# Scattering weighted expert results into one running sum instead of gathering them back by slot

## The reference

```python
xn = _layernorm(x, axis=-1)
x = x + attention(xn) + ffn(xn)
# ffn:
scores = einsum('btd,ed->bte', x, gate_w)
topk_scores, topk_idx = top_k(scores, 2)
topk_probs = softmax(topk_scores)
total_probs = sum(one_hot(topk_idx, E) * topk_probs[..., None], axis=-2)
h12 = einsum('btd,ehd->bteh', x, w12); h1, h2 = halves of h12
expert_out = einsum('bteh,edh->bted', silu(h1) * h2, w3)
y = sum(total_probs[..., None] * expert_out, axis=-2)
```

## Time and profile before

| | |
|---|---|
| median of 3 runs | 712.34 us (712.1 to 715.86) |
| the profiled execution | 713.24 us |
| its span, first to last instruction | 711.5 us |
| mean granted TensorE clock | 0.978 of full speed |
| batches 0 and 1, routing: until | 157.4 us |
| expert stage: until | about 514 us |
| attention of batches 2 to 7: until | 711.5 us |

### The profile page before, as it was taken

One profiled execution on the slowest core, in us unless ns is written; L12 is line 12 of the kernel. 1 busy time (PEld: TensorE's weight loads), 2 busy tenths in 40 slices (PEclk: granted clock), 3 DMA queues, 4 the chain that ended last, 5 costly groups with the idle time before them and its releaser, 6 DMA issues.

```text
span 711.5 us, 17988 instructions
## 1 busy us (share of the span) xinstructions
PE 633.2 (89%) x5916; PEld 512.0 (72%) x5917; DVE 571.6 (80%) x906; ACT 513.7 (72%) x883; POOL 280.4 (39%) x330
## 2 busy tenths in 40 slices
PE   0786776978999999999999999999889899999995
PEld 0564554754888888888888888888767676666673
DVE  4958899975688888888888888888687979788884
ACT  4554477474687787787777777777667788888885
POOL 3000273031344444444444444444300336666654
PEclk9998788998999999999999999999999999999999
DMA  9895477581111111111111111112168687885840
GB/s 300 268 257 174 128 262 273 146 284 31 49 53 52 59 52 52 59 53 50 59 55 50 57 56 51 56 54 56 45 161 258 174 259 180 271 227 161 215 138 30
DMA packets 66384, 92.74 MB, mean 130 GB/s; under 512 B 6448, under 2 KB 53424, under 8 KB 66320
## 3 DMA queue, kind: packets, MB, share of 16 engines
q1 hardware_dynamic: 57904, 70.56, 33.3%
q0 software_dynamic: 6864, 18.75, 7.9%
q10 hardware_dynamic: 1568, 2.76, 1.2%
HBM read 59.06 MB, written 32.83 MB: 129 GB/s over the span
## 4 chain that ended last, share of the span: by engine, by line
PE 63%; DVE 14%; ACT 10%; issue 8%; DMA 2%; POOL 2%; ACTq 0%; SPq 0%; DVEq 0%; POOLq 0%
PE PS L1300 55%; PE PS L1549 4%; DVE SMALL L964 4%; ACT WORK L781 3%; DVE XN L1122 2%; PE PS L1527 2%; DVE WALL L958 2%; ACT QS L776 1%; DMA XN<-in_x 1%; DVE WORK L1033 1%; DVE WORK L1026 1%; POOL OTS L595 1%; ACT WORK L719 1%; DVE WALL L982 1%; DMA KS<-parts_scratch 1%
## 5 line engine op out<-in xcount | busy, mean ns | idle before, releaser
L367 DVE TENSOR_TENSOR WS<-WALL,WS 128x1024 fp32r<-128x1024 f32 x136 | 166.9, 1227 | 56.0 <-ACT WS L862 41.5
L1300 PE MATMUL PS<-WS,XTS 128*128 128x512 f32 x804 | 203.9, 402 | 0.0
L1300 PEld LDWEIGHTS PS<-WS,XTS 128*128 128x128 f32 x804 | 146.2, 189 | 30.5
L862 ACT ACTIVATE WS<-WALL 128x1024 fp32r x136 | 143.7, 1056 | 9.1 <-issue 0.3
L1300 PE MATMUL PS<-DOWN_HIGH,HTS 128*128 x568 | 108.3, 290 | 5.0 <-DVE DOWN_LOW L958 3.5
L595 POOL TENSOR_TENSOR OTS<-SIDE,XN 128x256 f32<-128x256 f32 x31 | 23.8, 768 | 209.2 <-DVE XN L1122 142.2
L1300 PEld LDWEIGHTS PS<-DOWN_HIGH,HTS 128*128 128x128 f32 x568 | 86.4, 190 | 5.5 <-issue 5.5
L964 DVE TENSOR_REDUCE SMALL<-PS 128x8 f32<-128x1024 f32 x64 | 77.5, 1211 | 12.6 <-PE PS L1300 12.4
L781 ACT ACTIVATE WORK<-PS 128x512 f32<-128x512 f32 x128 | 69.4, 594 | 24.8 <-PE PS L1300 21.4
L658 POOL DMA_INDIRECT ys_scratch<-SIDE,SIDX x36 | 43.8, 1215 | 97.0 <-ACT SIDE L893 97.0
L654 POOL DMA_INDIRECT XS<-xn_scratch,GIDX x72 | 70.4, 978 | 23.6 <-issue 21.6
(11 more groups left out here) (148 smaller groups left out, 1094.8 us busy)
## 6 DMA issues: line engine op xcount, KB each, us to landing
WALL<-in_wexp SPq DMA_DIRECT2D x28, 384.0 KB, 7.1
WALL<-ys_scratch SPq DMA_DIRECT2D x16, 512.0 KB, 7.3
parts_scratch<-WORK SPq DMA_DIRECT2D x32, 240.0 KB, 2.5
QS<-parts_scratch SPq DMA_DIRECT2D x16, 480.0 KB, 4.6
XN<-in_x SPq DMA_DIRECT2D x4, 1024.0 KB, 12.1
xn_scratch<-XN SPq DMA_DIRECT2D x4, 1024.0 KB, 7.2
WALL<-in_x SPq DMA_DIRECT2D x8, 512.0 KB, 5.7
KS<-parts_scratch SPq DMA_DIRECT2D x16, 240.0 KB, 3.9
```

The source lines that it names most:

```text
L367: eng.tensor_tensor(out=WS[:, 1 - k, half, 1], in0=weights, in1=WS[:, 1 - k, half, 0].bitcast(F32), op=ALU.subtract).then_inc(low_ready[ha ...
L862: act.activation(WS[:, 1 - k, half, 0], weights, ACT.Copy).then_inc(high_ready[half], 1)
L1300: return pe.matmul(o, a, b, start=start, stop=stop)
```

## The change: what it does

- `xn_dram` rows become 258 wide: the two shares of a token stand behind its 256 features. ScalarE issues one transfer that writes them (8 bytes a token, 4096 tokens) in batch 0.
- `sum_dram` replaces `ys_dram`. SyncE copies x into it, from HBM to HBM, in 8 transfers of 512 KB: batches 0 and 1 behind `load_experts(1, 3)`, batches 2 to 7 behind `begin(1)` and ahead of `load_experts(LATE, E)`.
- The gather brings a token's two shares along; GpSimd picks the right one for each slot with two small instructions a tile (`find_share`), and `take_y` scales by it while it copies.
- The scatter adds into the token's row of `sum_dram`. Each waits until the one before it has landed, since both may add to one row.
- `keep(b)` moves from SyncE to GpSimd, as a transfer that adds the attention output of batches 0 and 1 into `sum_dram`.
- The last stage loads one row for each token of batches 2 to 7 and adds the bias to it (one GpSimd instruction a tile); ScalarE's `scale` and GpSimd's `combine` are gone. Batches 0 and 1 leave by one copy each from `sum_dram` to `out`.

```diff
@@ SyncE
-            def keep(b):
-                sp.wait_ge(r_free, (b + 1) * NWIN + 1)
-                sp.dma_start(rv[:, t, :], XN[:, t, :]).then_inc(rows_out, 16)
+            def copy_x(b):
+                r = slice(b * L, (b + 1) * L)
+                sp.dma_start(sum_dram[r], x[r]).then_inc(x_copied[b], 16)
             begin(0)
             load_experts(FIRST_EXPERTS, EARLY - 1)
+            for b in range(EXTRA):
+                copy_x(b)
             sp.wait_ge(early_done, 1)
             load_tokens(1)
             load_experts(EARLY - 1, LATE)
             begin(1)
+            for b in range(EXTRA, B):
+                copy_x(b)
             sp.wait_ge(map_done, 1)
             load_experts(LATE, E)
-            keep(0)
-            load_tokens(2)
-            keep(1)
+            load_tokens(EXTRA)
...
             def rest(b):
-                sp.dma_start(XR[:, t, :], xv[:, t, :]).then_inc(rest_in[b], 16)
-                for k in range(2):
-                    sp.dma_start(YG[:, t, k, :], yv[:, t, k, :]).then_inc(rest_in[b], 16)
+                sp.dma_start(XR[:, t, :], sv[:, t, :]).then_inc(rest_in[b], 16)
@@ GpSimd
+            def keep(b):
+                pool.wait_ge(r_free, (b + 1) * NWIN + 1)
+                pool.wait_ge(x_copied[b], 16)
+                pool.dma_start(sum_dram[...], XN[:, t, :], accum_op=ALU.add).then_inc(rows_out[b], 16)
             def own(b, n):
-                pool.wait_ge(own_scaled, 2 * ((b - OWN) * TB + n + 1))
-                pool.wait_ge(rest_in[b], 48)
-                combine(b * TB + n, BOUT[:], own_ready)
+                pool.wait_ge(rest_in[b], 16)
+                pool.tensor_tensor(out=XR[:, t, :], in0=XR[:, t, :], in1=BOUT[:], op=ALU.add).then_inc(own_ready, 1)
             def scatter(j):
-                pool.indirect_dma_start(ys_dram, ..., YS[j % 2], None)
+                if j:
+                    pool.wait_ge(y_out[1 - j % 2], 16 * ((j + 1) // 2))
+                else:
+                    (waits for all copies of x and both keeps)
+                pool.indirect_dma_start(sum_dram, ..., YS[j % 2], None, compute_op=ALU.add)
+            def find_share(j):
+                k = j % 2
+                pool.wait_ge(xs_in[k], 16 * (j // 2 + 1))
+                link(pool.tensor_tensor(out=PAIR[:], in0=XS[:, k, D:ROW], in1=KIND[:, j, :], op=ALU.mult))
+                pool.tensor_tensor(out=SHARE[:, k:k + 1], in0=PAIR[:, 0:1], in1=PAIR[:, 1:2], op=ALU.add)
+                pool.wait_ge(share_ready, j + 1)
@@ ScalarE
-                    if b in LATER and u % 2 == 0:
-                        scale(LATER[b] * TB + u // 2, LATER[b], later_scaled)
-                    if b >= OWN and u % 2 == 1:
-                        scale(b * TB + u // 2, b, own_scaled)
+                    if b == 0 and u == 5:
+                        act.dma_start(xn_dram...[:, :, D:ROW], PW[:]).then_inc(shares_out, 16)
-                    act.activation(YS[k], bank(7)[:, 0:D], ACT.Copy).then_inc(ys_ready, 1)
+                    act.wait_ge(share_ready, j + 1)
+                    act.activation(YS[k], bank(7)[:, 0:D], ACT.Copy, scale=SHARE[:, k:k + 1]).then_inc(ys_ready, 1)
```

More of the change, by code:

```diff
@@ L43 @@
 KT = 2 * NT
-DUMP_ROW = 2 * B * L
+DUMP_ROW = B * L
+ROW = D + 2
 EARLY = 4
@@ L58 @@
 EXTRA = 2
-OWN = 3
-LATER = {4: 2, 5: 0, 6: 1}
-FIRST_LATER = min(LATER)
 WU, WD = NC_D * 2 * FH, FC * D
@@ L331, in layer @@
         xt_full, xt_high, xt_free = sem("xt_full"), sem("xt_high"), sem("xt_free")
-        rows_out = sem("rows_out")
+        rows_out = [sem(f"rows_out{b}") for b in range(EXTRA)]
+        x_copied = [sem(f"x_copied{b}") for b in range(B)]
         high_ready = [sem("high_ready0"), sem("high_ready1")]
@@ L488, in _ @@
             begin(1)
+            for b in range(EXTRA, B):
+                copy_x(b)
             sp.wait_ge(map_done, 1)
             load_experts(LATE, E)
-            keep(0)
-            load_tokens(2)
-            keep(1)
-            sp.wait_ge(rows_out, 16 * EXTRA)
+            load_tokens(EXTRA)
+            for b in range(EXTRA):
+                sp.wait_ge(rows_out[b], 16)
             sp.wait_ge(y_stored, 1)
             sp.dma_start(KS[STK:DEEP, 1], KS[STK:DEEP, 0]).then_inc(hot_back, 16)
-            def send_later(n, b):
-                sp.wait_ge(later_ready, (n + 1) * TB)
-                t = slice(b * TB, (b + 1) * TB)
-                sp.dma_start(ov[:, t, :], XR[:, t, :]).then_inc(out_done, 16)
+            rest(EXTRA)
             for b in range(EXTRA, LAST):
@@ L507, in _ @@
                     load_tokens(b + 1)
-                if b + 2 in LATER:
-                    if LATER[b + 2] < EXTRA:
-                        rows_back(LATER[b + 2])
-                    else:
-                        rest(LATER[b + 2])
-                if b > OWN:
+                if b == EXTRA:
+                    for src in range(EXTRA):
+                        r = slice(src * L, (src + 1) * L)
+                        sp.dma_start(out[r], sum_dram[r]).then_inc(out_done, 16)
+                else:
                     send(b - 1)
-                    if b - 1 in LATER:
-                        send_later(b - 1 - FIRST_LATER, LATER[b - 1])
             send(LAST - 1)
-            send_later(LAST - 1 - FIRST_LATER, LATER[LAST - 1])
             for n in range(NWIN):
@@ L651, in _ @@
                 divide(w)
+            keep(0)
             def gather(j):
@@ L667, in _ @@
             divide(7)
+            find_share(0)
+            find_share(1)
             pool.wait_ge(xt_full, 1)
             gather(2)
+            keep(1)
             for j in range(SLOT_TILES):
@@ L675, in _ @@
                 scatter(j)
+                if j + 2 < SLOT_TILES:
+                    find_share(j + 2)
             for k in range(2):
@@ L680, in _ @@
                 for n in range(NWIN):
-                    if b in LATER:
-                        later(b, n)
-                    if b >= OWN:
-                        own(b, n)
+                    own(b, n)
                     if b * NWIN + n < B * NWIN - 1:
@@ L791, in sides @@
                 act.sem_inc(o_free, 1)
-            def scale(t, src, ready):
-                act.wait_ge(rest_in[src], 48)
-                for k in range(2):
-                    act.activation(YG[:, t, k, :], YG[:, t, k, :], ACT.Copy, scale=PW[:, k, t:t + 1]).then_inc(ready, 1)
             def part_of_places(i):
@@ L915, in _ @@
                     if j + 2 == EXACT_UP:
-                        act.wait_ge(rows_out, 16 * EXTRA)
+                        for b in range(EXTRA):
+                            act.wait_ge(rows_out[b], 16)
                     if split:
```

82 lines of the change are left out of this document (39 added, 43 removed).

## The result

| | before | changed |
|---|---|---|
| median | 713.44 us (712.1 to 715.86) | 729.21 us (727.69 to 731.59) |
| profiled execution, its span | 713.24, 711.5 | 729.56, 727.7 |
| mean granted TensorE clock | 0.978 | 0.968 |

The ratio is 1.022, with a 95% interval from 1.0178 to 1.0262. The forecast had the sign (slower, +4.8 us), but the loss is more than three times that, and 729.2 lies outside 707 to 727. Lines such as L635 are now lines of the changed kernel: L448 is `copy_x`, L635 the scatter, L624 the gather, L641 and L642 `find_share`, L877 `take_y`, L1515 the turn of `XS`, L574 `divide`, L588 `own`, L452 `rest`.

What follows compares the result with a forecast made beforehand. TensorE was busy 89% of the span, a mean over three stages with different limits. Terms 1.2 + 11.6 + 0 + 0 - 8 = +4.8 us on a 712.34 median gave about 717, range 707 to 727.

Steps and rivals of the forecast that it cites:

- Steps 1 and 2: Start: six copies of x ahead of the late experts' weights stall TensorE 11.6 us; the first stages' other additions cost 1.2.
- The term T: Start: time by which the six copies of x delay the late weights, taken as 14 us between 8.0 and 16.
- one direction's rate: Rival at the start: the copies run at 394 GB/s, 8.0 us, stall 5.6, total 711 us; chance 0.18.
- the stall: Start of the expert stage: TensorE waits for the late weights, 11.6 us, paid in full since nothing runs ahead.
- the slack of 2.4: Start: the late weights land at 155.1 us, 2.4 us before TensorE is there, so only delay beyond that stalls.
- Step 3: Expert stage: GpSimd's added share picking, the scatter's wait and the scaled `take_y` are all covered; tile stays 4.84 us, cost 0.
- the cover: Expert stage: an adding scatter lands after 3.7 us of a 4.84 us tile, leaving 1.1 us before its wait costs.
- the scatter's wait becomes the period: Rival in the expert stage: scatter landing over 4.8 us sets the tile time; at 5.5, +56 us, 773; chance 0.11.
- Step 4: Last stage: removing ScalarE's scalings and most GpSimd additions gives back 8 us, between 5 and 10.5.
- the price of the second pair in a window: Last stage: scaling two pairs instead of one costs 0.87 us a batch, charged for every pair; batches 3 to 6 give 6.1.
- the last stage gives little back: Rival in the last stage: only 3 us return because scalings merely hindered each other; +9.8, 722 us; chance 0.08.
- The three signs named for being wrong: Wrong if weights land before 160 us, a tile takes over 4.9 us, or batch 4 stays near 34.

Runs made afterwards that it cites:

- e2: Changed kernel with batch 0's adding transfer `keep(0)` issued behind the gather of tile 2; 726.48 us, ratio 1.0188.
- e4: Changed kernel with a scatter that overwrites its rows instead of adding, all waits kept; 724.56 us, ratio 1.0155.
- e9: Changed kernel, all copies behind late weights, both `keep` behind tile 2's gather, gather before scatter, batch 3's stores not awaiting the last scatter; 715.4 us, ratio 1.0025.
- e5: Changed kernel; SyncE stores batch 3's stacks without awaiting the last scatter, sum load behind first stores, batch 2's first `own` behind its `divide`; 722.94 us, ratio 1.0138.
- e6: Kernel before with the changed kernel's last stage, experts' results left out of the output; 709.21 us, ratio 0.9944.
- e3: Changed kernel with GpSimd's `find_share` and next gather ahead of the scatter in each tile; 727.21 us, ratio 1.0193.
- e13: e3 with `XS` padded so that both its buffers begin at a multiple of 64 bytes; 729.94 us, ratio 1.0235.
- e15: e9 with the `XS` padding of e13; 714.39 us, ratio 1.0009.

## Why the prediction was wrong

Its +4.8 was +16.2 between the profiled executions. By its own terms, with what each measured:

- **Steps 1 and 2, +12.8 forecast, +12.2 measured. Right in size, partly by luck.** The queue, the wait and the fact that nothing runs ahead of it were right: the weights of experts 6 and 7 end the wait, with the copies ahead of them. The term T was not. I took 14 us, nearer the upper bound, because reads and stores had not been seen to exceed 400 GB/s in sum. The copies alone cost 8.8 (e2), near one direction's rate (8.0), which was the rival to which I gave 0.18. Two other terms made up for it: `keep(0)` took 2.7 us, which I had put down as hidden under the stall and which was in it, on the same engines; and the first stages cost 2.5 instead of 1.2. So 14.0 less the slack of 2.4, and 0.6 from the landing to the first turn, are the 12.2. These are the sizes in one trace; `keep(0)` and the first stages are known to some 2 us. The Trainium skill (DMA: Bandwidth & Descriptors, the section on latency and other measured facts) gives 207 to 214 GB/s per direction for copies between HBM tensors, measured on tiles of 128 rows of 16 KiB that lie apart; by this T had been estimated as 14.7. For the whole pieces of 512 KB here this case shows more: 3.15 MB in 8.8 us are 358.
- **Step 3, 0 forecast, +2.7 measured, wrong.** A tile was to stay at 4.84 and is at 4.873 (2.3 us, cause open); and 1.4 us go with the waits for `XS`, which e4 does not have. The steps up to the first `take_y` and from it to the second are 0.9 us shorter, which leaves the 2.7 to within 0.1. For the waits the failed term is `find_share`, 0.7 us forecast: from the scatter's start to the gather's it added 1.8 (3.35 against 1.57), since the price of a small instruction was taken from a stretch without a scatter before it (0.24). By the terms given, the gather would have started at 304.6 and not at 304.9, which changes nothing. The scatter's landing was 3.7 forecast and is 3.7 to 4.0 in the changed kernel; what I left out is the 0.7 us of issue behind it, so that the cover is 0.2 to 0.5 us and not 1.1. The rival "the scatter's wait becomes the period" decided at 4.8; in the steady stretch it stayed away, and at the end of e9's stage the chain stood at 4.76.
- **Not in the forecast at all: the end of the expert stage, +4.6.** I wrote that the scatter waits for its predecessor and named what stands behind it on GpSimd, but not what waits for the last one: SyncE, with the whole supply of batch 3 behind it. Nothing follows that scatter to hide its landing. Nor did I ask what the load of the sum would do ahead of batch 3's stores. e5 takes both away, and 4.4 us of 4.9 come back; e4 leaves up to 2 of them to the load.
- **Step 4, -8 forecast, -3.4 measured, wrong in size.** I took the price of the second pair in a window (0.87 a batch) and charged the first pair the same. Batches 4 to 6 gave back 0.81, 0.35 and 1.01 instead of 1.73 each (0.87, 0.91 and 1.01 in e6), batch 3 0.2 instead of 0.9, and batch 7 with the end 1.0 instead of 2.4. The first pair had fitted into ScalarE's idle time. The remark that 31.22 busy in 32.2 would still fit was no evidence: the batch stands at 33.1 with ScalarE at 23.0, so something other than these two engines' busy time bounds it.

The rival "the last stage gives little back", at 3 with a chance of 0.08, was right, but to the 722 that it gave must be added the losses of step 3 and of the end of the expert stage, which no case held. The range failed for that reason: every case varied a term of the sum, and none allowed for a term that was not in it. The three signs named for being wrong all stayed silent: the weights landed after 160, a tile took 4.89 in the mean, and batch 4 took 33.2 and not near 34.

## What to carry to other kernels

When independent work is strung into a chain (here: each scatter waits for the one before), price the whole loop of landing and issue against the period, and then ask who waits for the last link, because there nothing hides it. Ask also what the change puts ahead of it on the queue. Two queues that both delay one start hide each other: undo both before you judge either. And a cost measured when a second piece of work was put into a slot says nothing about the first one.

## What the runs showed of the hardware

- A scatter that adds moves the same bytes as a plain one in twice the packets and twice the engine time (11056 packets and 34.5% against 5520 and 16.9% in 280 us), lands in 3.7 to 4.0 us instead of 2.4 to 2.6 (e4), and its instruction is 1.66 us long instead of 1.07 to 1.20.
- An adding transfer of 512 KB on GpSimd's queue took 17.4 us beside the copies and the weights and 6.5 later, beside less; a gather behind it took 16 us, against 6.2 in the kernel before.
- A GpSimd instruction on two numbers a partition took 0.21 us behind a plain scatter, 1.57 right behind an adding one and 0.53 where a tile's adding scatter came last (e3).
- Copies from HBM to HBM in pieces of 512 KB held up what stood behind them by 8.8 us for 3.15 MB, 358 GB/s (e2 against before, one trace each).
- Matmuls of the down product were 3 ns longer in the kernels with the changed expert stage (291 and 281 against 288 and 278), whatever part of it was taken out, and 2 ns longer with the padding of e13 to e15; the cause is open.
